# Deeper weight buffers in the down projection, and q-norm steps moved behind the V loop

## The reference

```python
q    = rmsnorm(x @ wq_a.T) @ wq_b.T            # 16 heads of 128 + 64 (rope)
kv   = x @ wkv_a.T                             # 512 compressed + 64 (rope), shared by the heads
kv_x = rmsnorm(kv[..., :512]) @ wkv_b.T        # per head: k_nope (128), v (128)
s    = softmax((q . k) / sqrt(192)) ; out = (s @ v) @ wo.T
x    = layernorm(x + out)
gate = silu((x @ w_gate) * s_gate) ; up = (x @ w_up) * s_up      # w_*: int8, 2048 x 8192
x    = layernorm(x + ((gate * up) @ w_down) * s_down)            # w_down: int8, 8192 x 2048
```

## Time and profile before

| | us |
|---|---|
| the runs shown: median (lowest, highest of 2) | 8669.81 (8559.64, 8779.99) |
| the profiled execution's own time | 8546.79 |
| its span (slowest core, 5; the eight lie between 8531.3 and 8545.2) | 8545.2 |
| from the start of head 0 to the start of the feed-forward block | 1073.5 to 5391 |
| feed-forward block, 4 token tiles | 5391 to 8545 |
| PE busy | 7526.6 (88%) |
| mean granted PE clock | 0.950 |

### The profile page before, as it was taken

The page is one execution under the profiler, slowest core; times in us unless marked ns, Lnnn a source line. Parts: engine busy times, 40 slices in busy tenths (PEclk is TensorE's granted clock), DMA queues, the critical chain, the costliest instruction groups (busy, mean ns, idle before and its releaser), DMA issues. The chain is left out here.

```text
span 8545.2 us, 113802 instructions; the slowest of 8 cores (8531.3 to 8545.2 us)
## 1 busy us (share of the span) xinstructions
PE 7526.6 (88%) x37936; PEld 2962.8 (35%) x37936; DVE 3979.8 (47%) x4829; ACT 3170.7 (37%) x3449; POOL 704.8 (8%) x1160
## 2 busy tenths in 40 slices
PE   7877999999999999999999969898799789979986
PEld 3334533332233333322333214343244334423432
DVE  2134577777887777788777755110111011011101
ACT  2203566666776666667666642100000000000000
POOL 0000000000000000000000000112211221121122
PEclk9988999999999999999999979999999999999998
DMA  4325500000000000000000034546744764575466
GB/s 70 68 66 99 86 14 9 10 10 9 8 7 5 10 10 9 10 8 7 5 10 8 3 74 173 170 153 197 221 163 153 224 199 151 174 221 178 153 194 200
DMA packets 329894, 756.42 MB, mean 89 GB/s; under 512 B 88323, under 2 KB 90371, under 8 KB 321029
## 3 DMA queue, kind: packets, MB, share of 16 engines
q0 software_dynamic: 235840, 609.59, 24.8%
q1 hardware_dynamic: 93510, 139.56, 5.0%
HBM read 490.36 MB, written 62.91 MB: 65 GB/s over the span
## 5 line engine op out<-in xcount | busy, mean ns | idle before, releaser
L972 DVE TENSOR_TENSOR lac_sb<-lac_sb,at_sb 128x1024 f32<-128x1024 f32 x2016 | 2469.6, 1225 | 244.4 <-ACT at_sb L939 37.5
L939 ACT ACTIVATE at_sb<-scp,bias_sb 128x1024 bf16<-128x1024 f32 x2048 | 2278.8, 1115 | 457.0 <-PE scp L922 282.5
L954 PE MATMUL avp<-at_sb,V_sb 128*128 128x512 bf16 x4096 | 1253.7, 389 | 53.6 <-DVE aob L982 41.7
L908 PE MATMUL scp<-qfn,kf_sb 128*128 128x512 bf16 x4096 | 1242.4, 385 | 23.1 <-ACT at_sb L939 22.8
L1303 PE MATMUL e_d<-e_wd,e_fuse 128*128 128x512 bf16 x2048 | 801.7, 391 | 291.3 <-DMA e_wd<-wd 216.5
L1255 PE MATMUL e_g<-e_h1t,e_gw 128*128 128x512 bf16 x4096 | 938.1, 383 | 77.6 <-DVE e_fuse L1273 31.2
L1273 DVE SCALAR_TENSOR_TENSOR e_fuse<-e_u,su_sb,e_silu 128x512 bf16<-128x512 f32 x256 | 191.9, 751 | 1613.3 <-ACT e_silu L1268 1613.3
L1260 PE MATMUL e_u<-e_h1t,e_uw 128*128 128x512 bf16 x4096 | 925.8, 379 | 0.0
L922 PE MATMUL scp<-qfp,k_pe 64*128 64x512 bf16 x2048 | 805.4, 393 | 0.0
L918 PE MATMUL scp<-qfp,k_pe 64*128 64x512 bf16 x2048 | 805.3, 393 | 0.0
L1307 PE MATMUL e_d<-e_wd,e_fuse 128*128 128x512 bf16 x2048 | 801.0, 391 | 0.0
(11 more groups left out here) (164 smaller groups left out, 5706.1 us busy)
## 6 DMA issues: line engine op xcount, KB each, us to landing
e_wd<-wd POOLq DMA_DIRECT2D x512, 512.0 KB, 3.8
e_gw<-wg POOLq DMA_DIRECT2D x256, 512.0 KB, 3.5
e_uw<-wu POOLq DMA_DIRECT2D x256, 512.0 KB, 4.2
xw<-x_full POOLq DMA_DIRECT2D x64, 512.0 KB, 5.3
d_xo<-x_own SPq DMA_DIRECT2D x16, 1024.0 KB, 9.0
h_sp<-d_h1b SPq DMA_DIRECT2D x16, 1024.0 KB, 3.9
e_h1r<-h_sp SPq DMA_DIRECT2D x16, 1024.0 KB, 9.4
out<-e_ob SPq DMA_DIRECT2D x16, 1024.0 KB, 4.8
```

The lines of the kernel that those rows point to most:

```text
L908: t.matmul(scp[idx % 2][:, o:o + wd], kf[:, ks * P:(ks + 1) * P], qfn[hb][:, q0 + o:q0 + o + wd], start=True, stop=False)
L939: exd.inc(sc.activation(atb[:, idx % 4, 0:HF], scp[idx % 2][:, 0:HF], AF.Exp, bias=bias[:, 0:1], scale=SCALE))
L954: mm = t.matmul(avp[:, o:o + wd], Vt[:, ks, :], atb[:, idx % 4, o:o + wd], start=(ks == 0), stop=(ks == NKS - 1))
L972: ladc.inc(v.tensor_tensor(lac[:, qh % 2, 0:HF], lac[:, qh % 2, 0:HF], atb[:, idx % 4, 0:HF], ALU.add))
```

## The change

In the attention stage the table is gone: the V loop stands alone, then all four q-norm blocks one after the other, then the bias steps. The instructions are the same, and on each engine only their order changes. In V groups 0 and 1 of the later heads PE gets one more wait, on the counter `pat`; nothing in the kernel raises it, so it is a wait for 0. In the feed-forward stage the ring of `e_wd` has five buffers and five semaphores instead of three.

```diff
+            for vg in range(S // 512):
...
+                if vg < 2:
+                    _w(t, kfe)
+                    if h >= 1:
+                        _w(t, pat)
...
+            qld.wait(v, 3 * (h + 1))
+            for qc in range(T // 512):
                 if qc < 2:
                     _w(v, k2m)
                 else:
...
-
-            def emit_qn_b(qc):
                 _w(t, vsq)
                 _w(t, k2d)
...
-            if NVG >= 3 * NQC + 4:
-                qn_sched = {}
-                for qc in range(NQC):
-                    qn_sched[3 * qc + 3] = [lambda qc=qc: emit_qn_a(qc)]
-                    qn_sched[3 * qc + 4] = [lambda qc=qc: emit_qn_b(qc)]
-                qn_sched[3 * NQC + 3] = [emit_bias]
...
-                if qn_sched:
-                    for fn in qn_sched.pop(vg, []):
-                        fn()
...
-        wdb = [alloc(f"e_wd{i}", [P, 2, 1024], BF16) for i in range(3)]
+        wdb = [alloc(f"e_wd{i}", [P, 2, 1024], BF16) for i in range(5)]
...
-        wdl = GDma(nc, "e_wdl", 3)
+        wdl = GDma(nc, "e_wdl", 5)
...
-                        if gli >= 3:
-                            _w(g, dnm, gli - 2)
-                        wdl.dma(g, wdb[gli % 3][:],
+                        if gli >= 5:
+                            _w(g, dnm, gli - 4)
+                        wdl.dma(g, wdb[gli % 5][:],
```

More of the change, by code:

```diff
@@ L805, in build_program @@
             emit_ones_k(S // 512 - 1)
-            def emit_qn_a(qc):
-                if qc == 0:
-                    qld.wait(v, 3 * (h + 1))
+            for vg in range(S // 512):
+                it = h * (S // 512) + vg
+                if it >= 2:
+                    _w(t, vve, it - 1)
+                if vg < 2:
+                    _w(t, kfe)
+                    if h >= 1:
+                        _w(t, pat)
+                for sl in range(4):
+                    for kc in range(4):
+                        mm = t.matmul(
+                            scp[vg % 2][:, sl * P:(sl + 1) * P],
+                            kv_c[:, kc, (vg * 4 + sl) * P:(vg * 4 + sl + 1) * P],
+                            wkvb[hb][:, kc, DN:256],
+                            start=(kc == 0), stop=(kc == 3))
+                vvm.inc(mm)
+                _w(v, vvm)
+                vve.inc(v.tensor_copy(
+                    Vt[:, vg * 4:(vg + 1) * 4, :],
+                    scp[vg % 2].ap()[:, 0:512].rearrange("p (sl f) -> p sl f", sl=4)))
+            qld.wait(v, 3 * (h + 1))
+            for qc in range(T // 512):
                 if qc < 2:
@@ L839, in emit_qn_b @@
                                          mstat[:, 3:4]))
[L841 to L856, removed]
@@ L858, in build_program @@
-            NVG = S // 512
-            NQC = T // 512
-            if NVG >= 3 * NQC + 4:
-                qn_sched = {}
-                for qc in range(NQC):
-                    qn_sched[3 * qc + 3] = [lambda qc=qc: emit_qn_a(qc)]
-                    qn_sched[3 * qc + 4] = [lambda qc=qc: emit_qn_b(qc)]
-                qn_sched[3 * NQC + 3] = [emit_bias]
[L866 to L886, removed]
-                if qn_sched:
-                    for fn in qn_sched.pop(vg, []):
-                        fn()
@@ L890, in build_program @@
[L890 to L894, removed]
+            _w(v, k2d)
+            if h >= 1:
+                _w(v, exd)
+            k2d.inc(v.tensor_tensor(mstat[:, 4:5], mstat[:, 0:1], mstat[:, 2:3],
+                                    ALU.mult))
+            _w(sc, k2d)
+            qsq.inc(sc.activation(mstat[:, 5:6], mstat[:, 4:5], AF.Sqrt,
+                                  scale=1.0404))
@@ L896, in build_program @@
+            _w(t, qsq)
+            _w(t, k2d)
+            k2m.inc(t.matmul(lp[:, 0:1], onesr_f[:], mstat[0:1, 5:6],
+                             start=True, stop=True))
+            _w(v, k2m)
+            bsd.inc(v.tensor_scalar(bias[:], lp[:, 0:1], -SCALE, B_OFF,
+                                    ALU.mult, ALU.add))
             cks = [(o, min(512, HF - o)) for o in range(0, HF, 512)]
@@ L1304, in build_program @@
                                          fuse[:, ic, tsl * P:(tsl + 1) * P],
-                                         wdb[gli % 3][:, ici, 0:512],
+                                         wdb[gli % 5][:, ici, 0:512],
                                          start=(ic == 0), stop=(ic == 63))
@@ L1309, in build_program @@
                                     fuse[:, ic, tsl * P:(tsl + 1) * P],
-                                    wdb[gli % 3][:, ici, 512:1024],
+                                    wdb[gli % 5][:, ici, 512:1024],
                                     start=(ic == 0), stop=(ic == 63))
```

## The result

The changed kernel against the kernel before: ratio 0.987, 95% interval 0.981 to 0.994, so it is faster by more than the measurement's doubt, and by less than 2%. Compared so, the changed kernel took 8432.8 to 8436.4 us in all executions but one (8505.8), and the kernel before 8546.8 in its profiled execution, 8550.3 and 8559.6 in two more.

What follows compares the result with a forecast made beforehand. The prediction took the down-projection's weight-load ring to be bound by latency. From a span of 8545.2 us, minus 238, plus 101 for longer heads, with small corrections, it forecast 8405 us, own range 8365 to 8450, wider range 8315 to 8540.

Steps and rivals of the forecast that it cites:

- What bound the kernel: Down-projection stages: 254 us of waiting for weights, three-buffer ring bound by latency; five buffers were to gain 238 us.
- The rate of the DMAs: Down-projection loads: five buffers need 304 GB/s; the DMAs were taken to carry it, having shown 399 GB/s.
- rival 1: Down-projection: DMAs become the bound at 294 GB/s, the gain falls to 109 us, 8537 us in all; chance 0.20.
- rival 3: Down-projection: landing time grows with queue depth, five buffers give nothing, moved q-norm steps cost 101 us: 8648 us; chance 0.05.
- The stall that stays: Down-projection, where out and e_h1r traffic meets the weight loads: 4 us of stall left to each stage, 16 us.
- The V loop without steps: Attention stage, V loop of each head: without q-norm steps 16.2 us instead of 21.3, 5.1 us saved.
- The chain: Attention stage, four q-norm blocks in sequence behind the V loop: wholly exposed, 10.9 us added per head.
- The clock term: Attention stage, lower PE clock in the chain and after it: +0.5 us a head, ends -3.4 and +5.0.
- The sum: Whole kernel: 238 us gained in down-projection, 101 us lost over 16 heads, giving 8405 us.
- The level: Whole kernel: predicted on the profiled execution's level, 8546.8 us, not the two timed runs' median of 8669.8.

Runs made afterwards that it cites:

- warm: The changed kernel with eight unused 512-column matmuls behind each of the four q-norm pairs and eight before the bias broadcast: 8374.6 and 8383.7 us.
- early: The kernel before with five e_wd buffers, q-norm steps two V groups earlier, bias product and root behind V group 12: 8268.8 us.

## Why the prediction was right and wrong

**What bound the kernel.** Right. 254 us of waits for weights and a ring bound by its latency were read from the rows; five buffers took 247 us from the stages, against 238 forecast.

**The rate of the DMAs.** Right: 311 GB/s in a steady stretch with no wait, so rival 1 (294 GB/s as a ceiling, worked out from the share) falls, and rival 3 with it: the median landing of e_wd is 3.8 us in both kernels. The Trainium skill (DMA: Bandwidth & Descriptors, "Where 436 GB/s comes from") puts what HBM gives one core at some 358 GB/s. No run here shows this limit or speaks against it: in that stretch the loads read half of what they write, 156 GB/s.

**The stall that stays.** 4 us a stage were left for the burst; the third sweeps lost 7 to 10 to waits. The prediction's own numbers say as much: transfers of 10.5 us less the 3.4 us that two more buffers hold are 7.1, not 4. Taken apart as the prediction did it, the stages were 883 + 70 + 254 + 61 us and are 883 + 70 + 34 + 34 now. So the waits fell by 220 us, 18 less than forecast, and the matmuls at the lower clock by 27, which the sum had left out but for a few us at its end. That 247 lies so near to 238 is luck in part.

**The V loop without steps.** Forecast 5.1 us shorter, measured 5.4 (21.4 to 16.0 from the first start to the last, mean over the heads).

**The chain.** Forecast 10.9 us more between V loop and broadcast, measured 12.1 (2.9 to 15.0). Of the 1.2, some 0.9 is the clock, which `warm` shows: in its ten heads with the clock up throughout the chain takes 14.1 us of the 15.0. There the pairs stand 2.75 us apart, near the 2.78 of the sum; at 0.50 they stand 3.16 apart (the timelines above).

**The clock term.** This is the term of the sum that had the wrong size. I weighed 1.6 us of cost in the chain against up to 3.4 us that the attention might get back, and took +0.5 a head. The clock cost some 0.9 us in the chain, and the attention got nothing back: its first exponential came another 0.7 us later behind the broadcast (2.9 before, 3.6 now), and it is 175.6 us long as before. So the clock cost 1.6 us a head where 0.5 stood. Summed over the records of the granted clock, it was at the lower level for 11.1 us of a chain and for 7.9 of the first 12 us of an attention, where the kernel before has 0.2 and 6.8 (means of 16 heads of core 5). The head as a whole is 7.6 instead of 6.3 us longer, 121 instead of 101 us in all, inside the bounds (38 to 173).

**The sum.** -238 + 101 = -137 us was forecast, -118 (the quickest runs, 8550.3 and 8432.8) to -123 (core 5) came, and on the level of the profiled execution 8405 us stands against 8432.8 to 8436.4, inside the forecast's own range (8365 to 8450).

**The level.** This is the step that failed. The number itself, 8405 us with a range up to 8540, missed the median of 8920.5 us. I took the level of the profiled execution, since nothing in the trace accounted for the upper of two timed runs (8780). A trace of another execution cannot account for it; with one of two runs so far up, the range had to reach there too. The runs showed the upper level to be the common one: 17 of the 19 runs of the kernel before took 8780 us or more, and 16 of the 22 of the changed kernel 8585 or more. Set against the median of the two runs, 8669.8, the forecast also read as 265 us less, where its own sum had 137. What makes most executions so much longer stays open.

## What to carry to other kernels

A ring of load buffers is bound by latency when (end of use to issue) + (issue to use) + (use), over the number of buffers, exceeds the time of use; here 6.37 us over 3 against 1.72. Count the spread of the landings as well: four buffers satisfied the sum and still left 40 us, and of the 37 us of waits that five left, 23 went away by moving other transfers out of the burst, not by depth. A chain of small steps that is hidden between matmul groups costs its whole latency when it is put in one piece (12.1 us a head here), the lower clock included, and more of the clock behind it; the better move is the other way, so that DVE and ACT finish while PE still has groups to run.

## What the runs showed of the hardware

- A DMA share of 1.04 at 311 GB/s with PE not waiting: the share is no ceiling, as a value above 1 says itself (the times of packets overlap in it). Scaling a rate by it (294 GB/s) gave a bound that the next run passed.
- In head 5 of the changed kernel the lower clock (0.50) came 2 us behind the V loop's last matmul and stayed for 17.1 us over a stretch in which PE ran eight sums, the broadcast and the first scores. Eight unused matmuls behind each pair kept it at 1.00 from the second pair on, and shortened the mean head by 3.1 us, though they held up the second pair by 1.3 us where the clock was already down.
- The clock at the start of the attention is worth 1.7 to 1.8 us of its length: first to last exponential is 175.6 us where it is at 0.50 for 7 to 8 of the first 12 us (the kernel before, the changed one), and 173.8 and 173.9 us where that is 2.1 and 0.6 us (`warm`, and core 3 of `early`).
- The landing time of the 512 KB loads does not depend on how many buffers they fill: medians of 3.8, 3.8 and 3.7 us with three, four and five.
